# New step orders in a three-kind transformer kernel, and the layer norm's scale and offset moved from the weights to the turned rows

## The reference

```python
h = shift_token(x)
mu = h.mean(-1, keepdims=True)
var = h.var(-1, keepdims=True)
h = (h - mu) / jnp.sqrt(var + 1e-05) * lg + lb
h = h @ w1 + b1
a, g = jnp.split(h, 2, axis=-1)
h = a * jax.nn.gelu(g, approximate=False)
x = x + h @ w2 + b2
...
x = _layernorm(x + _L0_attn_ref(x, ...), axis=-1)
x = _layernorm(x + _L0_ffn_ref(x, ...), axis=-1)
```

## Time and profile before

| | |
|---|---|
| median of 3 runs | 1886.77 us |
| lowest and highest | 1885.72 and 1888.03 us |
| profiled execution | 1886.66 us, its span 1885.1 us |
| mean granted clock of TensorE | 0.949 |
| busy: PE, DVE, ACT, POOL | 1759.3, 1144.2, 982.9, 864.0 us |
| matmuls | 14072 |
| moved by DMA | 121.29 MB, 64 GB/s |

### The profile page before, as it was taken

The page is one execution under the profiler, slowest core; times in us unless marked ns, Lnnn a source line. Parts: engine busy times, 40 slices in busy tenths (PEclk is TensorE's granted clock), DMA queues, the critical chain, the costliest instruction groups (busy, mean ns, idle before and its releaser), DMA issues. The chain is left out here.

```text
span 1885.1 us, 42756 instructions
## 1 busy us (share of the span) xinstructions
PE 1759.3 (93%) x14072; PEld 1335.8 (71%) x14072; DVE 1144.2 (61%) x2863; ACT 982.9 (52%) x1897; POOL 864.0 (46%) x886
## 2 busy tenths in 40 slices
...
GB/s 142 143 123 98 123 130 116 123 115 108 26 56 2 33 33 33 33 33 22 11 69 101 67 66 69 56 12 34 33 33 10 24 33 22 80 56 79 89 88 46
DMA packets 105656, 121.29 MB, mean 64 GB/s; under 512 B 23386, under 2 KB 78340, under 8 KB 105604
## 3 DMA queue, kind: packets, MB, share of 16 engines
...
...
## 5 line engine op out<-in xcount | busy, mean ns | idle before, releaser
L485 DVE TENSOR_REDUCE a_negm<-d 128x2 f32<-128x256 f32 (+3 forms) x256 | 201.1, 815 | 122.2 <-PE d L631 120.3
L448 ACT ACTIVATE a_PT<-b 128x384 f32<-128x384 f32 (+1 forms) x384 | 185.0, 524 | 135.6 <-PE b L670 69.7
L901 POOL TENSOR_TENSOR l_t<-l_t,l_t 128x512 f32<-128x512 f32 x128 | 165.4, 1293 | 148.3 <-DVE l_t L1053 147.3
L1071 DVE CUSTOM_DVE_ANT_0 d<-d,window 128x256 f32<-128x256 f32 (+1 forms) x512 | 184.3, 421 | 29.1 <-PE d L1171 29.0
L985 ACT ACTIVATE l_PT<-b 128x512 f32<-128x512 f32 (+1 forms) x256 | 125.4, 542 | 109.8 <-PE b L1213 106.3
L1479 POOL TENSOR_TENSOR m_hid_lo<-m_hid,m_hid_hi 128x512 fp32r<-128x512 f32 x80 | 105.1, 1323 | 154.7 <-ACT m_hid_hi L1537 154.5
L1099 PE MATMUL d<-w,l_xt 128*128 128x512 f32 x384 | 165.9, 432 | 3.2 <-DVE l_t L1053 2.3
L1100 PE MATMUL d<-w,l_xt 128*128 128x512 f32 x384 | 152.4, 397 | 0.0
L1101 PE MATMUL d<-w,l_xt 128*128 128x512 f32 x384 | 151.7, 395 | 0.0
L1205 PE MATMUL b<-l_Q,l_K 64*128 64x256 f32 x1536 | 140.3, 295 | 3.2 <-ACT l_PT L985 3.2
L919 POOL TENSOR_TENSOR l_zl<-l_zt,l_zh 128x512 fp32r<-128x512 f32 x64 | 85.7, 1348 | 120.4 <-ACT l_zh L991 120.4
...
## 6 DMA issues: line engine op xcount, KB each, us to landing
a_Q<-qk_parts SPq DMA_DIRECT2D x192, 64.0 KB, 2.1
a_K<-qk_parts SPq DMA_DIRECT2D x192, 64.0 KB, 2.1
...
```

What stands on the lines that cost most here:

```text
L448: nc.scalar.activation(PT[:, p // PG % 2, 2 * (p % PG) + hh, QOFF[t]:QOFF[t] + nq], SC[hh][:, 0:nq], ACT.Exp, scale=AD ** -0.5).then_inc(e ...
L485: dve.tensor_reduce(negm[:, q, 2 * p:2 * p + 2], MX[i % 2][:, :, 0:nk], AX.X, ALU.max, negate=True).then_inc(max_done, 1)
L901: pool.tensor_tensor(t1[:, par, w, :], t1[:, par, w, :], t2[:, par, w, :], ALU.add)\
L1071: m = dve.tensor_tensor_reduce(out=o, in0=o, in1=mask, scale=-1.0, scalar=-NEG, op0=ALU.add, op1=ALU.min, accum_out=negm[:, q + t, p // 2, ...
```

## The change

The tables have new orders. The feed-forward's `w` step is gone: its weights are split as they are, and the offset isn't added to the bias; instead `f_te` applies scale and offset to the turned rows, on ACT, once into the high part and once into a float32 copy `hf`, from which DVE subtracts the high part. `hf` lies where `hn` lay. `out` of the local attention is four steps in place of one, and the opening has a table of its own, in which `nw` (the loads of the next weights) comes before the last front steps.

The first attention's loop before and after:

```diff
     STEPS = parse("""
-        f_x:0 f_xe:0 sm:27 st:8 mt:2 f_qk:0 f_qk:1 f_qe:0 f_qe:1 f_qk:2 f_qe:2 st:9 f_load:0 pv:0 st:10 sm:28
-        sm:29 st:11 sm:30 st:12 ms:2 sm:31 z0:0 st:13 xr:0 st:14 mt:3 f_qk:3 ms:3 z1:0 f_load:1 pv:1 f_qe:3
-        f_sm:0 st:15 f_sm:1 f_sm:2 st:16 f_sm:3 st:17 ms:4 f_sm:4 st:18 f_sm:5 f_sm:6 st:19 f_sm:7 z2:0 st:20
-        st:21 f_sm:8 ms:5 z0:1 f_mt:0 st:22 f_load:2 f_sm:9 z1:1 z3:0 f_sm:10 st:23 f_sm:11 pv:2 ms:6 f_sm:12
-        f_sm:13 z2:1 f_st:0 ms:7 z0:2 f_sm:14 z1:2 f_sm:15 f_load:3 f_st:1 pv:3 z0:3 z3:1 f_v:0 f_st:2 z2:2
-        f_sm:16 f_sm:17 z1:3 f_mt:1 z3:2 f_v:1 z2:3 f_st:3 z3:3 f_sm:18 f_sm:19 f_st:4 f_v:2 out:0 f_sm:20
-        f_sm:21 f_ms:0 out:1 out:2 out:3 f_st:5 f_sm:22 f_sm:23 f_st:6 f_v:3 f_ms:1 f_sm:24 end:0 f_sm:25 f_st:7
-        f_sm:26""")
+        f_xe:0 f_x:0 sm:27 st:8 mt:2 f_qk:0 xr:0 f_qk:1 f_qe:0 sm:28 sm:29 f_qe:1 st:9 f_qk:2 st:10 f_load:1
+        f_qe:2 sm:30 ms:2 f_load:0 sm:31 st:11 pv:0 mt:3 st:12 f_qk:3 z0:0 z1:0 ms:3 st:13 f_sm:0 f_sm:1 st:14
+        f_sm:2 f_qe:3 f_sm:3 st:15 z2:0 pv:1 st:16 ms:4 f_sm:4 f_sm:5 ms:5 st:17 f_sm:6 f_sm:7 st:18 z0:1
+        f_sm:8 st:19 f_load:2 f_sm:9 st:20 f_sm:10 z1:1 z3:0 ms:6 ms:7 st:21 f_sm:11 f_sm:12 st:22 f_mt:0
+        f_sm:13 z2:1 f_sm:14 st:23 pv:2 z0:2 z1:2 f_sm:15 pv:3 z0:3 z3:1 z2:2 f_st:0 f_v:0 f_mt:1 f_st:1 z1:3
+        f_sm:16 f_sm:17 z3:2 f_ms:0 z2:3 f_v:1 f_st:2 z3:3 f_v:2 f_sm:18 f_st:3 f_sm:19 out:0 out:1 f_st:4
+        f_sm:20 f_sm:21 out:2 out:3 f_v:3 f_st:5 f_sm:22 f_sm:23 f_ms:1 f_st:6 f_sm:24 end:0 f_st:7 f_sm:25
...
+    OPENING = parse("""
+        f_xe:0 f_x:0 f_qe:0 f_qe:1 f_qk:0 f_load:0 f_qk:1 f_qk:2 f_qk:3 nw:0 f_sm:0 f_sm:1 f_sm:2 f_qe:2
+        f_load:1 f_qe:3 f_sm:3 f_sm:4 f_load:2 f_sm:5 f_sm:6 f_sm:7 f_sm:8 f_mt:0 f_sm:9 f_load:3 f_sm:10
+        f_sm:11 f_sm:12 f_st:0 f_ms:0 f_sm:13 f_st:1 f_sm:14 f_sm:15 f_v:0 f_sm:16 f_st:2 f_ms:1 f_sm:17
...
```

The feed-forward's loop:

```diff
-        f_n:0 w1:2 h:2 f_m:0 w2:0 w1:3 w2:1 w1:4 h:3 h:4 f_in:0 xr:0 f_t:0 w1:5 w2:2 h:5 w2:3 w2:4 f_te:0 w2:5
-        y:0 f_w1:0 f_h:0 f_w1:1 fin:0 f_h:1""")
+        f_n:0 w1:2 h:2 w2:0 w1:3 w2:1 f_m:0 w1:4 h:3 h:4 f_t:0 w1:5 f_te:0 w2:2 f_in:0 w2:3 h:5 f_w1:0 xr:0
+        f_w1:1 f_h:0 f_h:1 y:0 w2:4 w2:5 fin:0""")
```

The local attention's, of whose table the last two lines stand for the rest:

```diff
 ...
-        f_t:1 zs:1 z:2 f_te:1 st:7 zn:2 f_sm:1 f_t:2 pv:3 f_te:2 f_sm:2 ps:3 f_t:3 sv:3 f_te:3 f_sm:3 xr:0 zs:2
-        z:3 f_v:0 zn:3 zs:3 f_v:1 f_v:2 f_mt:0 f_v:3 out:0""")
 ...
+        f_sm:0 f_te:1 f_t:1 zn:2 ps:3 st:7 f_sm:1 f_t:2 zs:0 pv:3 f_te:2 f_sm:2 zs:1 zs:2 f_te:3 f_t:3 sv:3
+        f_sm:3 z:3 xr:0 f_v:0 zn:3 zs:3 f_v:1 f_mt:0 f_v:2 out:0 out:1 out:2 f_v:3 out:3""")
```

The first two joins, in part:

```diff
...
-        nwo:0 out:0 +f_qe:6 out:1 +f_qk:7 out:2 out:3 +f_qe:7 +f_iv:3 end:0 +pick:0 +set:0 ns:2 +f_t:0 +f_te:0 +f_sm:0
-        +f_t:1 +f_te:1 +f_sm:1 +f_t:2 +f_te:2 +f_sm:2 +f_t:3 +f_te:3 +f_sm:3 +f_v:0 +f_v:1 +f_v:2 +f_mt:0 +f_v:3
...
+        z2:2 z1:3 +f_iv:2 +f_qe:6 pv:3 z3:2 z2:3 +f_qk:6 +f_qe:7 +f_qk:7 +set:0 z3:3 out:0 out:1 +f_t:0
+        +f_iv:3 +f_te:0 out:2 +f_t:1 +f_te:1 out:3 +f_t:2 +f_te:2 nwo:0 +f_sm:0 +f_t:3 +f_te:3 end:0 +f_sm:1
...
-        +f_te:0 pv:1 st:5 ps:2 sv:1 z:1 nm:0 +w:0 st:6 zn:1 zs:0 ns:0 pv:2 sv:2 zs:1 z:2 st:7 zn:2 pv:3 ps:3 +set:0 sv:3
-        zs:2 ns:1 z:3 zn:3 zs:3 +f_w1:0 +f_w1:1 ns:2 out:0 +f_h:0 +f_h:1 +banks:0 +nw:0"""),
...
+        +f_te:0 z:3 pv:3 nw:0 xr:0 zs:3 zn:3 sv:3 +f_w1:0 out:0 +f_h:0 out:1 out:2 out:3 ns:2 +f_w1:1 +banks:0
+        +set:0 +f_h:1 +nw:0"""),
...
```

What the steps do, cut to its core:

```diff
     def high(self, act, n):
 
-        copy, gam = self.nc.scalar.activation, self.gam
+        copy = self.nc.scalar.activation
         if n < KT:
-            act.wait_ge(self.w_loaded, 32)
-            copy(self.w_hi[:, n, :], self.w_raw[:, n, :], ACT.Copy, scale=gam[:, n:n + 1]).then_inc(self.hi_done, 1)
+            act.wait_ge(self.w_loaded, 16)
+            copy(self.w_hi[:, n, :], self.w_raw[:, n, :], ACT.Copy).then_inc(self.hi_done, 1)
         else:
             act.wait_ge(self.mix_set, 2)
-            for k in range(KT):
-                copy(self.mix_hi[:, k, :], self.mix_raw[:, k, :], ACT.Copy, scale=gam[:, k:k + 1])\
-                    .then_inc(self.hi_done, 1)
+            copy(self.mix_hi[:, :, :], self.mix_raw[:, :, :], ACT.Copy).then_inc(self.hi_done, 1)
             act.wait_ge(self.w2_loaded, 64)
...
             elif name == "f_te":
+                if isinstance(b, int):
+                    act.wait_ge(own.loaded, 96)
+                else:
+                    act.wait_ge(w1_done, b * NT)
+                act.wait_ge(turned, b * KT + KT)
                 for k in range(KT):
-                    act.wait_ge(turned, b * KT + k + 1)
-                    if k == 0 and not isinstance(b, int):
-                        act.wait_ge(w1_done, b * NT)
-                    nc.scalar.activation(ht_hi[:, k, :], FB[k][:, :], ACT.Identity).then_inc(hi_done, 1)
+                    nc.scalar.activation(ht_hi[:, k, :], FB[k][:, :], ACT.Identity, scale=gam[:, k:k + 1],
+                                         bias=bet[:, k:k + 1])
+                    nc.scalar.activation(hf[:, k, :], FB[k][:, :], ACT.Identity, scale=gam[:, k:k + 1],
+                                         bias=bet[:, k:k + 1]).then_inc(scaled, 1)
...
-            if name == "w":
-
-                dve.wait_ge(bias_full, lay + 1)
-                dve.wait_ge(own.loaded, 80)
-                for k in range(2):
-                    dve.tensor_tensor(b1[:, k, 0:NF], b1[:, k, 0:NF], AB[0][0][:, NF * k:NF * k + NF], ALU.add)
-                dve.tensor_tensor(b1[0:TAIL, 0, NF:NT], b1[0:TAIL, 0, NF:NT],
-                                  AB[0][0][0:TAIL, 2 * NF:2 * NF + 1], ALU.add).then_inc(bias_done, 1)
-                dve.tensor_tensor(b1[AT:MIX, 1, NF:NT], b1[AT:MIX, 1, NF:NT],
-                                  AB[0][0][AT:MIX, 2 * NF:2 * NF + 1], ALU.add).then_inc(bias_done, 1)
-                dve.wait_ge(bias_done, 2 * lay + 2)
...
             elif name == "f_te":
                 for k in range(KT):
-                    dve.wait_ge(hi_done, b * KT + k + 1)
-                    dve.tensor_tensor(ht_lo[:, k, :], FB[k][:, :], ht_hi[:, k, :], ALU.subtract)\
+                    dve.wait_ge(scaled, b * KT + k + 1)
+                    dve.tensor_tensor(ht_lo[:, k, :], hf[:, k, :], ht_hi[:, k, :], ALU.subtract)\
                         .then_inc(lo_done, 1)
...
-            elif name == "w":
-                pe.wait_ge(*before.maxima)
-                pe.wait_ge(own.mix_set, 2)
-                pe.wait_ge(own.loaded, 80)
-                for c in range(2 * NF + 1):
-                    for f in range(KT):
-                        if c < 2 * NF:
-                            at = HID * (c // NF) + P * (c % NF)
-                            lhs, rows = w_raw[:, f, at:at + P], P
-                        else:
-                            lhs, rows = mix_raw[:, f, :], MIX
-                        m = pe.matmul(AB[0][0][0:rows, c:c + 1], lhs, bet[:, f:f + 1], start=(f == 0),
-                                      stop=(f == KT - 1))
-                m.then_inc(bias_full, 1)
```

More of the change, by code:

```diff
@@ L919, in do @@
                 pool.tensor_tensor(zl[:, i, :], zt[:, i, :], zh[:, i, :], ALU.subtract).then_inc(zl_done, 1)
-            elif name == "out" and not isinstance(b, int):
+            elif name == "out" and i == TB - 1 and not isinstance(b, int):
                 pool.wait_ge(y_done, b * TB + TB)
@@ L1081, in do @@
             elif name == "out":
[L1082 to L1089, removed]
+                if i == 0:
+                    dve.wait_ge(xr_in, b * 16 + 16)
+                    dve.wait_ge(own.ready, 16 * NB - 16)
+                    dve.wait_ge(own.last, 16)
+                    dve.wait_ge(stored, (b - base) * 16)
+                dve.wait_ge(y_full, b * TB + i + 1)
+                dve.tensor_tensor(out[:, i, :], YB[i % 2][:, 0:DM], xr[:, i, :], ALU.add).then_inc(y_done, 1)
             elif name == "ns":
@@ L1576, in do @@
                 n, rows = b * NT + i, P if i < NF else TAIL
+                if name == "f_w1" and isinstance(b, int):
+                    dve.wait_ge(own.loaded, 96)
                 dve.wait_ge(gate_done, n + 1)
@@ L1715, in tensor @@
         return do
-    left = Left(front=(lo_done, end * KT), maxima=(hid_done, end * NT - 1), scores=(hid_done, end * NT),
+    left = Left(front=(scaled, end * KT), maxima=(hid_done, end * NT - 1), scores=(hid_done, end * NT),
                 sums=(y_done, end * TB), queries=(w1_done, end * NT), values=(w1_done, end * NT),
@@ L1754 @@
-        +f_qk:1 +tab:0 +f_qe:1 w2:2 h:5 +f_iv:0 +f_qk:2 w2:3 +f_qe:2 +f_qk:3 w2:4 +f_qe:3 +f_iv:1 w2:5 +f_qk:4 nwo:0 y:0
-        +f_qe:4 fin:0 +f_qk:5 +f_qe:5 +f_iv:2 ns:2 +pick:0 +set:0 +f_qk:6 +f_qe:6 +f_qk:7 +f_qe:7 +f_iv:3 +f_t:0 +f_te:0
-        +f_sm:0 +f_t:1 +f_te:1 +f_sm:1 +f_t:2 +f_te:2 +f_sm:2 +f_t:3 +f_te:3 +f_sm:3 +f_v:0 +f_v:1 +f_v:2 +f_mt:0 +f_v:3
-        +banks:0"""),
```

(7 more changed lines are left out.)

104 lines of the change are left out of this document (50 added, 54 removed).

## The result

The changed kernel takes 1899.48 us (median of five runs, 1893.29 to 1902.39), the kernel before 1885.72 us beside it (1883.76 to 1888.03): a ratio of 1.0064, 95% interval 1.004 to 1.0087. It is slower by 13.8 us between the medians (12.0 between the means, which is what the ratio says), where I had forecast 24. The interval leaves out 1, so the loss is real, if small. The profiled execution took 1902.39 us, the longest of the five and 15.7 more than that of before.

The account below looks back on a forecast made before the run. The prediction took TensorE (PE), busy for 93% of the span, to bound the kernel. Its terms, led by +57 us in the attention loop, summed to +24 on 1886.7: 1911 us, range 1873 to 1942.

Parts of the forecast that it names:

- The local loops: Local attention: an ACT copy behind f_v:3 no longer covered by out, 0.35 us an iteration, 14 times: +5 us.
- The attention loop: f_load:1 queued on SP ahead of f_load:0 makes PE wait at f_sm:0: 8.1 us an iteration, seven times, +57 us.
- the upper bound of 70 for the clock: Attention loop: its cost can be +70 us if the granted clock falls after nine idle microseconds.
- Rival A: Attention loop: the order of the loads costs nothing, PE does not wait for their issue; 1854 us, chance 0.12.
- The opening: Start of the kernel: weights' loads behind f_qk:3, one store pair behind the first load; -2 us, from -6 to +3.
- Join 0: Front steps placed earlier shorten PE's waits, such as 6.52 us ahead of f_t:0; -9 us, between +2 and -16.
- Joins 1, 2 and 3: Joins 1 and 3: bias step gone, out ahead of ns:2, -16 us each; join 2: earlier front steps, -9 us.
- the bias step: Joins 1 and 3: the 44 matmuls of w per layer come off PE's path whole, -10 us.
- The feed-forward: Layer 0: f_te's extra ACT operations stall f_w1:0, +2.5 us; layer 1: subtraction from SBUF also meets POOL's add, +14.5 us.
- Rival B: Attention stalls as forecast, but layer 1's feed-forward subtractions do not meet POOL; 1895 us, chance 0.2.
- C: Attention stall costs 70 us through a lower clock, and the joins give back 25 in place of 50; 1944 us, chance 0.15.
- D: Denser tables win more in attention than the waits cost, loop grows by only 4 us; 1883 us, chance 0.13.

Follow-up runs that it names:

- Old_local: Changed kernel with the local attention's table of before, the four steps of out at its end; 1910.6 us in one run.
- swap_loads: Changed kernel with f_load:0 and f_load:1 exchanged in the attention loop's table; 1853.15 us, 0.9828 of the kernel before.
- before_loads: Kernel before, with f_load:1 put ahead of the third store pair and of f_load:0 in the attention loop; 1946.82 us in one run.
- Best: Changed kernel with the old attention loop, old feed-forward loop and the opening's old order; 1813.5 us, 0.9601 of the kernel before.
- old_join0: Changed kernel with join 0's table of before; 1919.94 us in one run.
- w_cut: Kernel before, with 40 of the bias step's 44 matmuls and two of its four adds left out per layer; 1869.62 us in one run.
- Xr_early: Changed kernel with xr (POOL's residual add and its loads) moved in the feed-forward loop from behind f_w1:0 to behind w2:1; 1954.76 us in one run.
- xr_late: Changed kernel with xr moved in the feed-forward loop from behind f_w1:0 to behind f_h:0; 1913.5 us in one run.

## Why the prediction was right, and where it was wrong

The sign, the place and the mechanism of the loss were right; its size as a whole was not, 24 us for 13.8. The step that failed is the term of the local loops, "0.35 us an iteration, 14 times: +5": the runs showed 12.2 us less in its place, with the other sign. The attention loop's +57 was too small by 12.5 us, and three smaller terms were off too.

- **The local loops**, +5 forecast, -12.2 measured. I looked at the one new neighbour (`f_v:3` ahead of `f_x`), whose copy turned out to be covered: PE does not wait at `f_x`. I let the reordered first half go at nothing, with PE at 99% and a clock of 1.00. Old_local shows 0.9 us an iteration from that order. Of this 0.34 us is a wait for DVE's maxima that is gone; the cause of the rest stays open.
- **The attention loop**, +57 forecast, +69.5 measured. The chain held nearly step by step: `f_load:1` from 12.9 us (12.05 forecast), `f_sm:0` at 27.8 (26.7). What let `f_load:1` go was not `st:11`, done about 11.1 us in, but the landing of the second store pair, whose last store is issued 10.6 us in and was at 9.4 before; I had put that at 11.8 at the latest. PE was ready 16.4 us in, before the 17 to 18.5 that I had, so its wait was 11.4 us and not 9. The term was mis-sized in two halves: `f_sm:0` came 1.1 us later, and behind it there were 40.4 us to the iteration's end where I had 39.3, at a clock that fell to 0.82. I had kept the upper bound of 70 for the clock and taken the middle. Rival A, the issue rate not mattering, is refuted by swap_loads and before_loads. The 50 ns a dispatch of the Trainium skill (DMA: Bandwidth & Descriptors, section Anatomy of one DMA) stood for that rival; the rows show 0.47 us an issue on average in every kernel run here.
- **The opening**, -2 forecast, +5.4 measured: I followed the first load and not `f_mt:0` behind `f_load:2`, which is the same question of SP's order that I had put first in the loop. Best shows 4.5 us back with the old order.
- **Join 0**, -9 forecast, -15.7 measured; old_join0 gives it to the join's table. I had halved a gain for which 25 us of idle stood in the row, for want of a count.
- **Joins 1, 2 and 3**, -16, -9 and -16 forecast, -16.1, -9.1 and -17.0 measured. Of the 16 the bias step is 9 to 10 (w_cut), as forecast. No run tests the other 6 to 7, nor the parts of join 2, so there only the sums are known to be right.
- **The feed-forward**, +2.5 in layer 0 exact; layer 1 +14.5 forecast, +11.1 measured, `f_w1:0` late by 1.5 us in place of 1.9. Xr_early and xr_late show its cause: 0.69 us a subtraction alone, 2.38 for two beside the add. That agrees with what the Trainium skill says of DVE instructions with two SBUF inputs (GPSIMD Engine Reference, section Key points). I had read from the rows that only the subtractions beside the residual add would be slow. The changed kernel shows it elsewhere too: in join 1, one at 1020.94 took 1.79 us beside two other POOL instructions with inputs in SBUF. Rival B is refuted; it had also taken off 16 us for a term of 14.5 in all.
- **The other rivals.** C had the attention loop right (69.5 us, under its 70, at a clock of 0.82) and the joins wrong: they gave back 57.9 us and not 25. Its sum should have been 1911 + 13 + 25 = 1949 by its own terms. D is refuted: the loop grew by 10 us an iteration, not 4.

Five terms were off by 3 to 17 us, in both directions, and the sum was nearer than they were; that is luck. The sign hung on the attention loop's error too: with that loop at +57 and all other stages as measured, the table's sum would be +3.5 us, less than the 3.8 us up to which I had called it no change.
